# The edge stage of a graph layer: each gather waits for a step of VectorE's round, and the second layer's small products go out in four parts

## The reference, cut to what matters

```python
Q = (h @ Wq).reshape(n, H, HD); K = (h @ Wk)...; V = (h @ Wv)...      # n = 3125, H = 8, HD = 32
score = jnp.einsum('ehd,ehd->eh', Q[dst], K[src]) / np.sqrt(HD)
score = score + jax.nn.relu(efeat @ W1 + b1) @ W2 + b2                # efeat: 64 features, 256 hidden, 8 heads
m = jax.ops.segment_max(score, dst, num_segments=n)
ex = jnp.exp(score - m[dst])
denom = jax.ops.segment_sum(ex, dst, num_segments=n)
alpha = ex / denom[dst]
out = jax.ops.segment_sum(alpha[:, :, None] * V[src], dst, num_segments=n)
```

## Time and profile before

| | us |
|---|---|
| median of 3 runs | 3579.12 (3571.62 to 3589.3) |
| the profiled execution: its span, first to last instruction | 3141.0 |
| PE busy over the span | 2529.7 (81%) |
| VectorE busy | 2313.5 (74%) |
| GpSimd busy | 1412.5 (45%) |
| ScalarE busy | 1278.8 (41%) |
| the 784 gathers (L1107), GpSimd busy | 833.0 |
| the 3038 records of small products (L1351), each | 0.27 |

### The profile page before, as it was taken

How to read it: one execution, slowest core, us unless ns; L and a number is a source line. 1 busy time by engine, 2 the same in 40 slices (tenths; PEclk the granted TensorE clock), 3 DMA queues, 4 the chain that set the end, 5 groups by cost and what they waited for, 6 DMA issues and landing times. The chain is left out here.

```text
span 3141.0 us, 61552 instructions
## 1 busy us (share of the span) xinstructions
PE 2529.7 (81%) x18415; PEld 1852.7 (59%) x18415; DVE 2313.5 (74%) x4036; ACT 1278.8 (41%) x2919; POOL 1412.5 (45%) x1363
## 2 busy tenths in 40 slices
PE   0895999999999999999363999678989999967058
PEld 0453655565555566566342556468989998966035
DVE  8554888888888888887463776688999999937601
ACT  0342555555555555555020111264544444533011
POOL 4686776767767676674333080251000000034251
PEclk9997999999999999999775999888999999988579
DMA  6327999999999999996223432100000000011040
GB/s 156 71 82 214 275 272 274 267 264 266 266 272 272 267 268 264 276 264 185 46 83 100 131 103 75 49 22 14 11 10 12 9 11 10 11 49 49 25 138 25
DMA packets 252154, 428.58 MB, mean 136 GB/s; under 512 B 58711, under 2 KB 162496, under 8 KB 251875
## 3 DMA queue, kind: packets, MB, share of 16 engines
q0 software_dynamic: 91920, 235.61, 27.4%
q1 hardware_dynamic: 156736, 185.86, 20.6%
q10 hardware_dynamic: 3344, 5.11, 0.5%
HBM read 508.04 MB, written 155.53 MB: 211 GB/s over the span
## 5 line engine op out<-in xcount | busy, mean ns | idle before, releaser
L1107 POOL DMA_INDIRECT edge_kv<-scratch_kv,edge_idx x784 | 833.0, 1063 | 342.7 <-issue 211.5
L1451 PE MATMUL edge_ps_o<-edge_vals,edge_onehot 128*128 128x264 f32 x1568 | 438.7, 402 | 29.3 <-ACT edge_rows L1316 19.8
L2889 PE MATMUL msg_ps_o<-all_fp,msg_at 125*123 125x256 bf16 x3375 | 434.5, 277 | 19.0 <-ACT msg_at L2942 15.7
L1316 ACT ACTIVATE edge_rows<-edge_ps_o 128x264 f32<-128x264 f32 x784 | 292.8, 392 | 291.1 <-PE edge_ps_o L1451 278.6
L1132 DVE TENSOR_TENSOR edge_prod<-edge_ps_q,edge_kv 128x512 f32<-128x512 f32 x392 | 257.5, 687 | 180.1 <-PE edge_ps_q L1366 166.6
L2889 PEld LDWEIGHTS msg_ps_o<-all_fp,msg_at 125*123 125x123 bf16 x3375 | 371.3, 137 | 25.3 <-ACT msg_at L2942 18.7
L1451 PEld LDWEIGHTS edge_ps_o<-edge_vals,edge_onehot 128*128 128x128 f32 x1568 | 258.8, 189 | 192.9 <-ACT edge_rows L1316 139.9
L1241 ACT ACTIVATE edge_hid<-edge_ps_h,edge_b 128x512 f32<-128x512 f32 x392 | 248.2, 685 | 177.7 <-PE edge_ps_h L1335 177.7
L1366 PE MATMUL edge_ps_q<-edge_qw,edge_slots 128*128 128x256 bf16 x2352 | 294.7, 276 | 14.2 <-DMA edge_qw<-scratch_qc 13.5
L2914 POOL TENSOR_TENSOR msg_x<-msg_x,msg_b 125x256 f32<-125x256 f32 x25 | 31.2, 1246 | 610.8 <-PE msg_ps_n L2865 610.8
L1366 PEld LDWEIGHTS edge_ps_q<-edge_qw,edge_slots 128*128 128x128 bf16 x2352 | 217.0, 99 | 123.5 <-issue 87.3
(11 more groups left out here) (525 smaller groups left out, 4279.6 us busy)
## 6 DMA issues: line engine op xcount, KB each, us to landing
edge_qw<-scratch_qc SPq DMA_DIRECT2D x980, 192.0 KB
scratch_part<-edge_rows SPq DMA_DIRECT2D x196, 396.0 KB
scratch_part<-edge_rows SPq DMA_DIRECT2D x196, 132.0 KB
edge_ef<-in_edge_t_dram SPq DMA_DIRECT2D x98, 256.0 KB, 4.5
edge_sgb<-scratch_seg SPq DMA_DIRECT2D x98, 256.0 KB, 5.9
ffn_w<-in_L_ffn_w_dram SPq DMA_DIRECT2D x18, 1024.0 KB
edge_kv<-scratch_kv,edge_idx POOLq DMA_INDIRECT x784
scratch_kv<-tab_kvrow SPq DMA_DIRECT2D x25, 250.0 KB
```

The lines of the kernel that those rows point to most:

```text
L1107: pool.indirect_dma_start(kv[p][:, t, :], None, K.kv_d, bass.IndirectOffsetOnAxis(ap=idx[p][:, t:t + 1], axis=0)).then_inc(rows_in[p][q], 16)
L1316: act.activation(rows[q % 2][:, t, :], ps_o[t % 2][:, 0:RW], ACT.Copy).then_inc(row_ready, 1)
L1451: pe.matmul(ps_o[t % 2][:, 0:RW], onehot[q % 2][:, t, :], vals[q % 2][:, t, :], start=True, stop=True).then_inc(out_done, 1)
L2889: m = pe.matmul(ps_o[gl % 3][0:GR, 0:D], at[gl % 3][:, h, :], K.fp[:, h, k, :], start=h == 0 and k == 0, stop=h == NT - 1 and k == 2)
```

## The change

GpSimd's wait moves into the loop over tiles. Of the four gathers of a quad the first keeps its wait; the second also waits for the first half of `products` of the round in which `vals` of quad W is made, the third for that round's `sums`, the fourth for the one-hot of the next round. Groups 0 and 1 don't wait. On PE, `scores(G, half)` becomes `scores(G, half, k)`, which waits for its own activation and does the four (in half 0, k = 0: one full and three small) products of that k. In the round of quad 1, half 0's k = 0, 1 stand where all four stood, and k = 2, 3 come before the third output product, ahead of the hidden products there. In the round of quad 2, half 1's k = 0 stands where all four stood, k = 1 behind the queries, k = 2 before the second output product and k = 3 before the fourth.

```diff
@@ GpSimd @@
                     for q in range(NQ):
-                        wait(pool, vals_ready, (G - 2) * NQ + q + 1)
-                        pool.nop(nofuse=True)
+                        W = (G - 2) * NQ + q
+                        paced = ((vals_ready, W + 1), (prod_ready, 2 * (W + AHEAD) + 1),
+                                 (sc_ready, W + AHEAD + 1), (hot_ready, W + 2))
                         for t in range(q * QT, (q + 1) * QT):
+                            if not isinstance(G, int) or G > 1:
+                                pool.wait_ge(*paced[t % QT])
+                                pool.nop(nofuse=True)
                             pool.indirect_dma_start(kv[p][:, t, :], None, K.kv_d,
...
@@ PE: the function @@
-            def scores(G, half):
-
-                pe.wait_ge(hid_ready, 8 * G + 4 * half + 4)
-                if half == 0:
+            def scores(G, half, k):
+
+                c, par = k // 2, k % 2
+                i = 2 * half + par
+                first = half == 0 and k == 0
+                pe.wait_ge(hid_ready, 8 * G + 4 * half + k + 1)
+                if first:
                     wait(pe, st_ready, G)
                     pe.matmul(ps_s[:, 0:EW], w2f[:], hid[:, 0, 0, 0, :], start=True, stop=False, skip_group_check=True)
-                for c in range(KC):
-                    for par in range(2):
...
+                for b in range(1 if first else 0, 4):
+                    pe.matmul(ps_s[32 * b:32 * (b + 1), 0:EW], w2s[:, c, (3 - i) * H:(3 - i) * H + 32],
+                              hid[:, c, b, par, :], start=False, stop=False, skip_group_check=True)
@@ PE: the round @@
                         if more and q == 1:
-                            scores(G + 1, 0)
+                            scores(G + 1, 0, 0)
+                            scores(G + 1, 0, 1)
                         if more and q == 2:
-                            scores(G + 1, 1)
+                            scores(G + 1, 1, 0)
...
                             queries(X, (q + 1) % NQ, G + 1 if q < NQ - 1 else G + 2)
+                        if more and q == 2:
+                            scores(G + 1, 1, 1)
...
                         for t in range(QT):
+                            if t == 2 and more and q == 1:
+                                scores(G + 1, 0, 2)
+                                scores(G + 1, 0, 3)
+                            if t == 1 and more and q == 2:
+                                scores(G + 1, 1, 2)
+                            if t == 3 and more and q == 2:
+                                scores(G + 1, 1, 3)
                             if t == 2 and more and q < 2:
                                 hidden(G + 1, q, 2)
                                 hidden(G + 1, q, 3)
```

More of the change, by code:

```diff
@@ L1337, in hidden @@
                           start=True, stop=True).then_inc(hid_done, 1)
-            def scores(G, half):
-                pe.wait_ge(hid_ready, 8 * G + 4 * half + 4)
-                if half == 0:
+            def scores(G, half, k):
[4 more added lines that the diff above has]
+                if first:
                     wait(pe, st_ready, G)
                     pe.matmul(ps_s[:, 0:EW], w2f[:], hid[:, 0, 0, 0, :], start=True, stop=False, skip_group_check=True)
-                for c in range(KC):
-                    for par in range(2):
-                        i = 2 * half + par
-                        for b in range(4):
-                            if half == 0 and c == 0 and par == 0 and b == 0:
-                                continue
-                            pe.matmul(ps_s[32 * b:32 * (b + 1), 0:EW], w2s[:, c, (3 - i) * H:(3 - i) * H + 32],
-                                      hid[:, c, b, par, :], start=False, stop=False, skip_group_check=True)
+                for b in range(1 if first else 0, 4):
+                    pe.matmul(ps_s[32 * b:32 * (b + 1), 0:EW], w2s[:, c, (3 - i) * H:(3 - i) * H + 32],
+                              hid[:, c, b, par, :], start=False, stop=False, skip_group_check=True)
             def query_scores(G):
@@ L1409, in _ @@
                 pe.wait_ge(w2_in, W2_IN)
-                scores(0, half)
+                for k in range(4):
+                    scores(0, half, k)
             for X in range(NQ):
```

## The result

The changed kernel took 3385.17 us (median of 4, 3384.8 to 3391.85), the kernel before 3575.76 us (median of 4, 3571.62 to 3589.3): ratio 0.9463, 95% interval 0.9436 to 0.9491. The forecast was 3588 us, with 3546 to 3618 as its range. Not even the sign was right.

The account below looks back on a forecast made before the run. The edge stage was bound by a ring of PE through quads 0 to 2, then briefly VectorE. Small products +10.6 us, gathers -1, so +9 on the median 3579 gave 3588 us; range 3546 to 3618.

Parts of the forecast that it names:

- Against which time: Whole kernel: the 438 us between profiled span and median lie around the span, unchanged, so 9 is added to 3579.
- part one: GpSimd's gathers, each held to a step: costs nothing, gains 1 us through window loads, bounds 0 and -3.6 us.
- Part two, half 0: PE, quad 1: no wait for the last hidden product, extra entry and exit for the split; -0.20 us per group.
- Part two, half 1: PE, quad 2: four single parts around queries and between outputs, 3.86 us for 3.21; +0.65 us per group.
- the 0.23 wait for `vals`: PE before quad 3's outputs: VectorE's `vals` come 0.7 to 0.8 us earlier, so this 0.23 us wait goes.
- The sum: PE to quad 3's outputs: +0.45 less 0.23, +0.22 us per group; 48 groups +10.6 us, less 1 for gathers.
- What the prediction said would show it: Six blocks, shorter VectorE waits in quads 1 and 2, no idle before L1344, outputs 1.32 behind queries, pair 49.3 + 0.4.
- (a): Rival, faster: parts slip into PE's stalls at little cost, VectorE's earlier round decides; 3544 us full, 3561 half; chance 0.25.
- (b): Rival, slower: PE's array empties between strip and full products, short blocks pay each time; 3617 at 0.10 us; chance 0.22.
- (c): Rival, slower: the last gather lands late and stops VectorE; 3627 us for the first us beyond 12; chance 0.03.
- (d): Rival: pacing finds nothing to improve and both parts cancel; no change, 3579 us; chance 0.5 together with the forecast.

Follow-up runs that it names:

- e1: The kernel before, run again without an edit on a quick chip: 3144.23 us against 3144.92, ratio 0.9997.
- h1: Kernel before with one wait per relu in place of one for four, small products still in one block per half group; slow chip: 3640.48 us against 3642.34.
- h2: Kernel before with one wait per relu, small products unspread, plus the change's waits on the gathers; slow chip: 3419.05 us against 3642.34, ratio 0.9373.
- g1: Kernel before with only the first half group's small products in parts, gathers as before; quick chip: 3123.44 us against 3143.72, ratio 0.9925.
- g2: Kernel before with only the second half group's products in parts, and four waits for the first half's block; quick chip: 3121.59 us against 3143.72, ratio 0.9924.
- i1: Kernel before with gathers from the third group on replaced by plain transfers of consecutive rows; slow chip: 3185.28 us against 3634.15, ratio 0.8769.

## Why the prediction was wrong

**The step that failed is "Against which time", and with it the term of part one.** The prediction put the 438 us between span and median outside the span, as start and end of the program; e1 measured 1.8 us there. The difference lies in the stage itself: h1's last output product on a slow chip ends at 1975.9 us, before's in the profile at 1496.0, which is 480 of the 507 us between these two spans. There the gathers hold the other engines, so the term for the gathers, taken as -1 us with bounds of 0 and -3.6, was -221 us on a slow chip (h2 against h1). Profile and times of before were of different executions, 438 us apart, and every price was read where the mechanism that decided the result does not occur. A span 12% below the median of three runs could have warned.

**Part one, the gathers.** Forecast: nothing, at best -3.6, by better windows. On quick chips it is +8.6 to +11.5 alone; in the whole change the windows' 2.8 us in 943 fall to 0.2 to 0.5, and the whole change is 5.5 and 6.8 us below the small products alone. That the gathers land in time was right: no VectorE wait on them. On slow chips the term is -221 us. No row of the trace before could give its size, or its sign: the gathers stand there as close to each other (0.30 us between them) and hold nobody. The Trainium skill, page "DMA: Bandwidth & Descriptors", section "Queues, rings and completion order", has each DMA engine go round robin over its queues, from which the prediction had the bursts delay the windows and pacing repair it. The runs agree with that inference for pacing beside the small products (0.2 to 0.5 us of waiting) and contradict it for pacing alone, 11.2 us instead of 3.5.

**Part two, half 0.** Forecast -0.20 us a group. Measured from the earlier trace rows and the timeline above, output pair to hidden product, plus the part in the middle of quad 1: 2.86 became 1.88 (812.02 to 813.90) plus 0.58 (817.26 to 817.84), -0.40. The wait gave 0.45 (forecast 0.34), and the distance from the full product to the first small one (L1344 to L1351 before, L1351 to L1353 now) fell from 0.42 to 0.32, which was not in the sum; splitting the block cost 0.57 + 0.58 - 1.00 = 0.15, as forecast (0.14).

**Part two, half 1.** Forecast +0.65 less the 0.23 wait for `vals`, +0.42. Measured from the block's start to L1358: 4.53 before, 825.97 - 820.85 = 5.12 after, +0.59; L1358 to the queries 0.22 where it was 0.33, and outputs 1.31 behind them, not 1.55, and 0.09 less from there to L1375 (2.93 where it was 3.02). Together +0.15. A part takes 0.36 to the next instruction, the forecast's 0.34. The sizes that were off: 0.06 in the block itself, and 0.11 behind L1358 (its two records last 0.38, not 0.49) and 0.09 behind the outputs, which were not in the sum. Why PE is faster there was not tried.

**The sum.** -0.25 a group by these, -0.28 in the groups, where +0.22 was forecast: over the forecast's 48 groups -13 us instead of +10.6. With the windows -17.2 and -19.0 us were measured on quick chips. So on a quick chip, too, the sign of the forecast is wrong, by 26 to 29 us, though the change is only some 0.6% there. What the prediction said would show it held in part: six blocks, the idle before L1344 gone, outputs 1.31 behind the queries, VectorE's wait in quad 2 0.57 instead of 1.06. A pair takes 48.76 us, not 49.3 + 0.4. VectorE's wait in quad 1 did not get shorter (2.44 in the group shown, 2.20 before): its queries come 0.99 us earlier in the group, but VectorE is ready 1.24 us earlier.

**The rivals.** (a) had the sign and part of the mechanism for quick chips, but not its cause, the single wait for four relus. (b) did not occur: a single part between outputs costs 0.36 + (823.62 - 822.98) less two output passes of 0.22, which is 0.56 us, where the rows gave 0.54, so entry and exit have the 0.1 each that the rows had. An estimate from the Trainium skill, page "TensorE: Matmul & The Clock Gate", section "Single matmul latency", with its fixed 0.166 us (for bf16) at both ends, would make this 0.54 - 0.19 + 0.33 = 0.68; the trace decides for 0.56. (c) did not occur. (d) is excluded on both kinds of chip, on quick ones narrowly (0.9949, 95% interval 0.9933 to 0.9966). None of them held what decided the result: that gathers in a row hold up the other engines.

## What to carry to other kernels

Before a sum is made on a profile, its span is laid beside the runs' times; if they differ by far more than the 2 us seen here, the profile shows another way of running, and a forecast from it is good for that one alone. A wait for the last of several results in front of work that could start with the first costs even where the work stays in one block: here 0.54 us a group, while spreading a half group's products cost about 0.15. Indirect gathers in a row are worth breaking up even where no engine waits for them, since on some chips they stop the others: the changed kernel is 0.5 to 0.6% better on quick chips and 5.4% in the first result. On quick chips g1 and g2 (3123.44 and 3121.59) were better still, without any wait on the gathers; h2 (0.937 of before) was the best on a slow one among kernels that compute the layer.

## What was not expected of the hardware

Six chips ran the same kernel before with medians of 3142 to 3146 us (four) and 3555 to 3642 us (two); no execution of it lay in between. On the second kind ScalarE and VectorE start up to 6.0 us after PE's record has ended (h1; idle up to 8.3) while GpSimd issues indirect gathers 1.25 us apart, and behind the sixth gather in a row PE can advance in steps of 1.44 us; with plain transfers of the same bytes by the same engine this is gone (3185 us), with half the bytes it is not (3562 us). The Trainium skill, page "SBUF — State Buffer", section "SBUF: two separate sides", says that only VectorE shares a port with GpSimd and that PE and ScalarE never wait on anyone there; the traces of the slow chips have both held up together with VectorE, so what holds them is something else than that port, and what makes a chip slow stays open. The granted clock over the stage's window was lower too, 0.88 in h1 and 0.93 in the changed kernel against 1.00 in the earlier trace rows: an estimate from these is that TensorE ran at 1.2 GHz, the lower of its two levels, for 2 x 0.12 x 943 = 226 us in h1 and 132 in the changed kernel. In i1, on a slow chip with plain transfers, it was 1.00. So the lower clock is no property of the chip but came with the holding; what part of the 221 us it carries was not separated.
